# Attention scores from two float32r levels in 64 rows of the array, with neighbouring products in opposite row halves

## The reference, cut to what matters

```python
q = (x @ Wq.T + bq).reshape(B, S, H, Dh).transpose(0, 2, 1, 3)   # 16 heads of 16
scores = jnp.einsum('bhqd,bhkd->bhqk', q, k) / math.sqrt(Dh)
# + slope of the head * (key - query), causal mask, softmax, @ v, @ Wo
```

## Time and profile before

| | us |
|---|---|
| median of 3 runs | 5928.72 |
| lowest, highest | 5915.18, 5933.72 |
| span of the profiled execution | 5916.1 |
| first attention's steps (`ba`) | 833 to 1700 |
| second attention's steps (`ea`) | 3325 to 5150 |

### The profile page before, as it was taken

One profiled execution on the slowest core, in us unless ns is written; L12 is line 12 of the kernel. 1 busy time (PEld: TensorE's weight loads), 2 busy tenths in 40 slices (PEclk: granted clock), 3 DMA queues, 4 the chain that ended last, 5 costly groups with the idle time before them and its releaser, 6 DMA issues. The chain is left out here.

```text
span 5916.1 us, 82750 instructions
## 1 busy us (share of the span) xinstructions
PE 5058.1 (85%) x29088; PEld 2711.9 (46%) x29088; DVE 3390.4 (57%) x6345; ACT 2567.7 (43%) x5102; POOL 1828.3 (31%) x1800
## 2 busy tenths in 40 slices
PE   6566489999978566499987999999999999799996
PEld 3455333333325455357973333333333333255896
DVE  7511468887846721241119788878888878343111
ACT  2311217776662311132215176766766766513221
POOL 2388311111101288534331122222222222104332
PEclk9778779999989687699998899999999999889998
DMA  3476561222213277606986411221221221120798
GB/s 107 116 148 149 138 171 33 62 58 68 62 53 104 76 156 151 149 26 212 330 269 198 108 37 40 63 49 40 64 47 40 64 48 40 55 69 1 267 318 268
DMA packets 503528, 659.28 MB, mean 111 GB/s; under 512 B 147310, under 2 KB 358318, under 8 KB 497998
## 3 DMA queue, kind: packets, MB, share of 16 engines
q1 hardware_dynamic: 370158, 500.99, 27.0%
q0 software_dynamic: 133056, 154.15, 13.2%
HBM read 489.33 MB, written 164.20 MB: 110 GB/s over the span
## 5 line engine op out<-in xcount | busy, mean ns | idle before, releaser
L1724 DVE TENSOR_REDUCE ea_mx<-ea_psA 128x1 f32<-128x512 f32 (+3 forms) x2304 | 1373.9, 653 | 242.0 <-PE ea_psA L1585 144.1
L1706 ACT ACTIVATE ea_pr<-ea_psB 128x512 f32<-128x512 f32 (+3 forms) x2560 | 1198.9, 535 | 567.4 <-PE ea_psB L1608 557.7
L1585 PE MATMUL ea_psA<-ex_kx,ex_qx 99*128 99x512 bf16 (+3 forms) x2560 | 868.4, 357 | 20.2 <-DVE ea_mx L1724 13.3
L1608 PE MATMUL ea_psB<-ex_qx,ex_kx 99*128 99x512 bf16 (+3 forms) x2560 | 846.2, 349 | 0.0
L1724 DVE TENSOR_REDUCE ba_mx<-ba_psA 128x1 f32<-128x512 f32 (+3 forms) x1152 | 686.2, 653 | 144.3 <-PE ba_psA L1585 95.6
L1706 ACT ACTIVATE ba_pr<-ba_psB 128x512 f32<-128x512 f32 (+3 forms) x1280 | 601.5, 536 | 288.9 <-PE ba_psB L1611 155.5
L1625 PE MATMUL ea_psO<-ea_pr,ea_vx 128*32 128x512 f32 (+3 forms) x5120 | 603.5, 543 | 20.9 <-POOL ea_pr L1554 14.0
L1585 PEld LDWEIGHTS ea_psA<-ex_kx,ex_qx 99*128 99x128 bf16 x2560 | 250.3, 98 | 551.8 <-DVE ea_mx L1724 427.8
L1585 PE MATMUL ba_psA<-bx_kx,bx_qx 108*128 108x512 bf16 (+3 forms) x1280 | 443.5, 364 | 7.8 <-PEq L1146 4.5
L1608 PE MATMUL ba_psB<-bx_qx,bx_kx 108*128 108x512 bf16 (+3 forms) x1280 | 424.9, 349 | 14.6 <-DMA bx_qx<-ba_mT 14.4
L1608 PEld LDWEIGHTS ea_psB<-ex_qx,ex_kx 99*128 99x128 bf16 x2560 | 246.5, 98 | 310.3 <-ACT ea_pr L1706 141.0
(11 more groups left out here) (528 smaller groups left out, 8260.9 us busy)
## 6 DMA issues: line engine op xcount, KB each, us to landing
de_wg<-in_L_rg SPq DMA_DIRECT2D x64, 512.0 KB, 4.7
de_wu<-in_L_ru SPq DMA_DIRECT2D x64, 512.0 KB, 5.9
de_wd<-in_L_rd SPq DMA_DIRECT2D x64, 512.0 KB, 7.3
fe_wg<-in_L_rg SPq DMA_DIRECT2D x64, 512.0 KB, 4.9
fe_wu<-in_L_ru SPq DMA_DIRECT2D x64, 512.0 KB, 5.9
fe_wd<-in_L_rd SPq DMA_DIRECT2D x64, 512.0 KB, 7.5
ae_w<-in_L_w SPq DMA_DIRECT2D x64, 384.0 KB, 3.6
ce_w<-in_L_w SPq DMA_DIRECT2D x64, 384.0 KB, 3.8
```

The source lines that it names most:

```text
L1585: last = nc.tensor.matmul(psA[:, slot, at:at + n], qx[0:KB, s, hh, t * P:(t + 1) * P], kx[0:KB, s, hh, k:k + n], start=True, stop=not diag)
L1608: last = nc.tensor.matmul(psB[:, slot, off:BLK], kx[0:KB, s, hh, kt * P:(kt + 1) * P], qx[0:KB, s, hh, Q * BLK + off:(Q + 1) * BLK], start ...
L1706: nc.scalar.activation(pr[:, j % 4, hh, off:BLK], psB[:, exp_slot(n), off:BLK], ACT.Exp).then_inc(s_exp, 1)
L1724: v.tensor_reduce(out, src, AX.X, ALU.max).then_inc(s_ar, 1)
```

## The change

- q and k are split in two float32 values instead of three bf16: `lev[0]` is written by ACT as float32r, `lev[1]` is the rest. Three pairs of levels make 48 rows (`KP`). The bias takes 6 rows in `ba`, 2 in `ea`: 54 and 50 rows.
- Heads lie in row halves: head hh has the rows from `hh % 2 * 64` and the column block `hh // 2` of `qx` and `kx`. Both products of a head are float32r matmuls over 54 or 50 rows that start at row 0 or 64.
- The order of heads is 1, 3, 0, 2 for B (`HEAD_ORDER`) and 0, 2, 1, 3 for A; two heads that share an item are h and h + 2, which lie in the same half.
- Every mask is two matmuls over 64 rows instead of one over 128.
- The maxima get two levels: DVE's chain has 3 instructions instead of 5; the transpose and its copy are float32.
- `load_queries` has 8 DMAs a step; `load_keys` 8 in `ba`, 6 in `ea` (8 in its first two steps).
- The constants `c_q`, `c_k`, `c_q1`, `c_k1` become float32 and are copied from input to scratch in DRAM at the start of the program, on SP's queue behind x and the other constants. `first_operands` on POOL waits for these copies.

```diff
-LEVEL_PAIRS = ((0, 0), (0, 1), (0, 2), (1, 0), (1, 1), (2, 0))
-KP = len(LEVEL_PAIRS) * DH
+Q_LEVELS, K_LEVELS = (0, 0, 1), (0, 1, 0)
+KP = len(Q_LEVELS) * DH
+HALF = P // 2
...
-        lev = sc.sb("lev", [P, NL, 3, BLK], BF16)
+        lev = sc.sb("lev", [P, NL, 2, BLK], F32R)
...
-                    nc.vector.tensor_tensor(res[:, u, :], t32[:, u, :], lev[:, v, 0], ALU.subtract).then_inc(s_c, 1)
-                    dve.wait_ge(s_c, base + n * 2 + 1)
-                    nc.vector.tensor_copy(lev[:, v, 1], res[:, u, :]).then_inc(s_c, 1)
-                    dve.wait_ge(s_c, base + n * 2 + 2)
-                    nc.vector.tensor_tensor(lev[:, v, 2], res[:, u, :], lev[:, v, 1], ALU.subtract).then_inc(s_lo, 1)
+                    nc.vector.tensor_tensor(lev[:, v, 1], t32[:, u, :], lev[:, v, 0].bitcast(F32),
+                                            ALU.subtract).then_inc(s_lo, 1)
...
-            out += [(t, k0, m, (h, h + 1)) for h in (0, 2)] if m <= BLK // 2 else [(t, k0, m, (h,)) for h in range(HV)]
+            out += [(t, k0, m, (h, h + 2)) for h in (0, 1)] if m <= BLK // 2 else [(t, k0, m, (h,)) for h in (0, 2, 1, 3)]
...
+HEAD_ORDER = (1, 3, 0, 2)
...
 def load_queries(eng, op, st, s, signal):
...
+    for half in range(2):
+        at = half * HALF
+        signal(eng.dma_start(op.qx[at:at + op.F, s].bitcast(F32), op.constant(op.qc, st, half)))
+        at += op.F
+        for level in Q_LEVELS:
+            signal(eng.dma_start(op.qx[at:at + DH, s].bitcast(F32), level_rows(op.lvq, level, st, half)))
+            at += DH
...
                 def maxima(i, s, slot):
...
-                        last = nc.tensor.matmul(psA[:, slot, at:at + n], qx[0:KB, s, hh, t * P:(t + 1) * P],
-                                                kx[0:KB, s, hh, k:k + n], start=True, stop=not diag)
+                        r0 = hh % 2 * HALF
+                        last = nc.tensor.matmul(psA[:, slot, at:at + n], qx[r0:r0 + KB, s, hh // 2, t * P:(t + 1) * P],
+                                                kx[r0:r0 + KB, s, hh // 2, k:k + n], start=True, stop=not diag)
                         if diag:
-                            last = nc.tensor.matmul(psA[:, slot, at + n - P:at + n], C["identb"], C["maskA"],
-                                                    start=False, stop=True)
+                            for x in range(2):
+                                last = nc.tensor.matmul(psA[:, slot, at + n - P:at + n], C[f"identb{x}"][r0:r0 + HALF],
+                                                        C[f"maskA{x}"][r0:r0 + HALF], start=False, stop=x == 1)
...
                 def scores(j, hh, st, s, first):
...
+                    head = HEAD_ORDER[hh]
+                    r0, diag = head % 2 * HALF, r >= 0 and not two
+                    last = nc.tensor.matmul(psB[:, slot, off:BLK], kx[r0:r0 + KB, s, head // 2, kt * P:(kt + 1) * P],
+                                            qx[r0:r0 + KB, s, head // 2, Q * BLK + off:(Q + 1) * BLK],
+                                            start=True, stop=not diag)
...
+            for n, dst in kept.items():
+                sp.dma_start(dst.rearrange("r j s -> r (j s)"), D[n].rearrange("r j s -> r (j s)")).then_inc(s_kept, 16)
...
+def two_levels(a):
+
+    a = np.asarray(a, np.float32)
+    top = (a.view(np.uint32) & np.uint32(0xFFFFF000)).view(np.float32)
+    return top, a - top
```

More of the change, by code:

```diff
@@ L14 @@
 BF16 = mybir.dt.bfloat16
+F32R = mybir.dt.float32r
 I32 = mybir.dt.int32
@@ L1368, in load_keys @@
-def load_keys(pool, op, st, s, signal):
[L1369 to L1378, removed]
+        self.of_step = of_step
@@ new lines, in __init__, with keys_in, keys_after, constant @@
+        self.NQ = 2 * len(Q_LEVELS) + 2
+    def keys_in(self, st):
+        return 2 * len(K_LEVELS) + (2 if st < 2 or self.of_step else 0)
+    def keys_after(self, st):
+        return sum(self.keys_in(n) for n in range(2 - st % 2, st + 1, 2))
+    def constant(self, a, st, half):
+        return a[ds((st * 2 + half) * self.F, self.F)] if self.of_step else a
+def level_rows(lv, level, st, half):
+    if len(lv) == 2:
+        return lv[half][level, ds(st * (2 * DH), 2 * DH), :].rearrange("(j d) s -> d j s", d=DH)
+    return lv[0][level, ds(st * (HV * DH), HV * DH), :].rearrange("(j q d) s -> q d j s", q=2, d=DH)[half]
@@ new lines, in load_queries @@
+def load_queries(eng, op, st, s, signal):
+    for half in range(2):
[5 more added lines that the diff above has]
+            at += DH
+def load_keys(pool, op, st, s, signal):
+    for half in range(2):
+        at = half * HALF
+        if st < 2 or op.of_step:
+            signal(pool.dma_start(op.kx[at:at + op.F, s].bitcast(F32), op.constant(op.kc, st, half)))
+        at += op.F
+        for level in K_LEVELS:
+            signal(pool.dma_start(op.kx[at:at + DH, s].bitcast(F32), level_rows(op.lvk, level, st, half)))
+            at += DH
@@ L1607, in scores @@
                     slot = exp_slot(n)
-                    last = nc.tensor.matmul(psB[:, slot, off:BLK], kx[0:KB, s, hh, kt * P:(kt + 1) * P],
-                                            qx[0:KB, s, hh, Q * BLK + off:(Q + 1) * BLK], start=True, stop=two or r < 0)
-                    if r >= 0 and not two:
-                        last = nc.tensor.matmul(psB[:, slot, off:off + P], C["identb"], C["maskB"],
-                                                start=False, stop=True)
+                    head = HEAD_ORDER[hh]
[3 more added lines that the diff above has]
+                                            start=True, stop=not diag)
+                    if diag:
+                        for x in range(2):
+                            last = nc.tensor.matmul(psB[:, slot, off:off + P], C[f"identb{x}"][r0:r0 + HALF],
+                                                    C[f"maskB{x}"][r0:r0 + HALF], start=False, stop=x == 1)
                     last.then_inc(s_b, 1)
@@ L1982, in bf16 @@
     return np.asarray(a, np.float32).astype(mybir.dt.np(BF16))
-def three_levels(a):
-    a, out = np.asarray(a, np.float32), []
-    for _ in range(3):
-        out.append(bf16(a))
-        a = a - out[-1].astype(np.float32)
-    return out
-BIAS_ROWS, BIAS_MAX = 12, 3
+def two_levels(a):
+    a = np.asarray(a, np.float32)
+    top = (a.view(np.uint32) & np.uint32(0xFFFFF000)).view(np.float32)
+    return top, a - top
+BIAS_ROWS = 6
 F32_CONSTS = (("ident", P), ("code", NT), ("dummy", 1), ("ecol1", E0), ("lower", NG0 * NG0), ("rev1", E1),
```

123 lines of the change are left out of this document (53 added, 70 removed).

## The result

The changed kernel takes 6050.89 us (median of 4 runs, 6047.87 to 6073.81) beside 5930.74 us of the kernel before on the same chip: 1.0227 times as long, 95% interval 1.0207 to 1.0248. Forecast were 5705 us. From the first V group to the last, `ba` takes 846.9 us instead of 850.6 and `ea` 1855.8 instead of 1738.9: of the 132 us by which the two profiled executions differ (6047.8 and 5916.1), 117 lie in `ea`'s steps. (Before, `ba`'s last V group ends at 1738 us; the 1700 in the table of times is where its A items end.)

What follows compares the result with a forecast made beforehand. PE was taken to set the pace at 110.4 us a step, DVE 16 to 18 us behind. Steps 229 us less, copies +10, projections -5: 224 less than 5928.7, so 5705 us; range 5580 to 6110, likeliest case 5600 to 5800.

Steps and rivals of the forecast that it cites:

- the sum of a step: Attention steps: PE work, edges and lockstep give 100.5 us in `ea`, 101.6 in `ba`, from 110.4; 229 us less in all.
- what would make it wrong: Signs against the forecast, among them the granted clock (0.99 in middle steps) falling once DVE is level with PE.
- The halves run at once: A and B products in opposite row halves overlap: columns occupy 47.4 us a step in `ea`, 53.9 in `ba`.
- A float32r column: Both products: one float32r instruction of 512 columns takes 0.215 us, like bf16; upper end 0.86.
- no overlap: Rival, attention steps: halves do not overlap, masks and edges remain, +131 us, 6060 us; chance 0.18.
- dear columns: Rival, both products: float32r costs more than bf16; at 0.43 us for 512 columns +880, 6810 us; chance 0.12.
- the estimated 1.54: Speedup of two row halves by the Trainium skill's share: 70% of the overlap's saving, 5755 us; left out of the sum.
- a load waits for the product of its own half: Rival, products' weight loads: a pair takes 0.215 + 0.112 us, about half the overlap lost, 5850 us; chance 0.13.
- PE and DVE in lockstep: Attention steps, three banks: DVE holds PE up, adding 4 us a step in `ea` and 2 in `ba`.
- Edges: PE's steps: three more shape changes a step, in and out, at M's transposes: 6 x 0.095 us, 0.6 us.
- Masks: PE's steps: each mask becomes two in one half, adding 3.5 us a step in `ea`, 6.9 in `ba`.
- Outside: Outside the steps: constant copies at the start cost 10 us, projections gain 5 us.

Runs made afterwards that it cites:

- Clean (5): Changed kernel with GpSimd's scaling in the second attention at unit 25 instead of 14, merges from unit 28 instead of 23: 5918.95 us, ratio 0.9996.
- 3: Changed kernel with the second attention's scaling at unit 21 and every product and mask reading rows 0 to 63, so no opposite halves: 8752.69 us.
- 2: Kernel before, with the second attention's inverses one unit earlier (9 instead of 10) so that GpSimd's scaling meets DVE's chain: 5916.32 us, ratio 0.9996.
- 9: Kernel before, with GpSimd's scaling in the second attention at unit 21 and merges from unit 25: 5905.38 us, ratio 0.9972.
- 12: Changed kernel, scaling still at unit 14, products over all 64 rows of their half, the added rows zeros: 5983.88 us, ratio 1.0100.
- 13: Clean, with products over all 64 rows of their half, the added rows zeros: 5900.0 us, ratio 0.9968.
- 8: Kernel before, in bf16, both products over only the first 54 (ba) or 49 (ea) of their rows: 8264.64 us.
- 6: Clean, with each mask again one bf16 product over 128 rows instead of two over 64: 7394.69 us, ratio 1.2478.
- 10: Clean, with two V groups together in every second unit instead of one in every unit: 6248.78 us, ratio 1.0553.
- 11: Clean, with the order of heads 0, 2, 1, 3 for B as for A: 5984.85 us, ratio 1.0092.
- 4: Changed kernel with scaling at unit 21, plus a final phase of 48 wait-free products of each kind: float32r 512 columns 0.227 us, opposite halves 0.113 to 0.118.
- 7: Clean, with DVE reducing only every second column of the scores: 5760.61 us, 158 less than clean.

## Why the prediction was wrong

**Two things failed.** The result lies 346 us above the forecast. Clean (5) lies 214 us above it, with hardly a fall of the clock: the sum of a step at full clock was too low. The other 132 us go with the falls of the clock and the waits ahead of them, which the sum left out; they turned a change that was worth nothing into a loss.

**The failed step that made it slower is the clock.** The sum of a step multiplied columns by prices at full clock, as the earlier trace rows had it at 0.99, and named a fall only among what would make it wrong, with DVE level with PE as the reason. What the runs show instead: the change halves the rows that a column works in (50 of 128, 99 before), and without the overlap (3) the clock is at 1.2 GHz throughout. With the overlap a wait of 1.3 to 3.3 us goes with 14 to 55 us at 1.2 GHz, where one of 2.5 to 3.9 us cost the kernel before 3 to 7 (2 and above), and one of 1.2 to 2.3 us nothing (2, 9). Waits of 1.3 us or more also come in nine steps of fourteen instead of five, since DVE's chain now meets GpSimd's scaling more often. Take the waits away (5) and the ratio falls from 1.0227 to 0.9996, 132 us between the medians; keep the waits and give every product more rows (12) and it falls to 1.0100, 67 us; do both (13) and the clock stays full. Half rows in bf16 (8), without a wait, stood at 1.2 GHz for most of the attention. Waits aren't the only occasion: in 6, 10 and 11 the clock falls with none of 1 us. What brings it down there no run took apart. The trace of before held the pieces: four falls behind waits, and DVE's chain held for 4.5 us once. I looked at means of five steps, not at the low stretches.

**Right.** The halves run at once, fully in 4, and pairs start 0.01 us apart in the kernel. A float32r column costs what the prediction took, plus 5%. So the rivals of no overlap and of dear columns fall. That the former named 6060 us, 9 from the result, is chance: its mechanism isn't there. Two halves give 2.0 (0.227 to 0.1135 us in 4), not the estimated 1.54. The 5755 us worked out from it leave out the 4 and 2 us for lockstep that 5705 holds; with them it would have been 5835. That a load waits for the product of its own half (the Trainium skill, "TensorE: Matmul & The Clock Gate", "The mechanism") is not so in a running stream: 0.227 us in one half with loads between. At the start of a burst a load does seem to show, below.

**Mis-sized at full clock.** Clean steps are 107.4 and 108.0 us where the sum gave 100.5 and 101.6. Most steps of `ea` before that have no long wait take 108.5 to 109.9 us from V group to V group, so at full clock 1 to 2 us are left of the 9.9 forecast. With DVE's work halved (7) the steps take 100.9 and 103.2, where PE's own sum gave 96.5 and 99.6: some 4 us of each step were missing in PE's work, and 2.5 to 3 in the lockstep.
- *PE and DVE in lockstep*, taken as 4 and 2 us: cutting DVE's work gives 6.5 and 4.9 back (7). The clean step has DVE at 85%. No run cut DVE's work in the kernel before, so how much of this it paid already isn't known.
- *Edges*, taken as 0.6 us. PE of the clean kernel in order of time, two pairs, a V group, and the pairs behind it:

```profile
4000.42 0.49 PE L1594 MATMUL ea_psA<-ex_kx,ex_qx 50*128 50x512 f32 x1 [0.32 <-DVE ea_mx L1738]
4000.43 0.49 PE L1620 MATMUL ea_psB<-ex_qx,ex_kx 50*128 50x512 f32 x1
4000.85 1.07 PE L1639 MATMUL ea_psO<-ea_pr,ea_vx 128*32 128x512 f32 x8
4001.84 0.50 PE L1594 MATMUL ea_psA<-ex_kx,ex_qx 50*128 50x512 f32 x1
4001.85 0.73 PE L1620 MATMUL ea_psB<-ex_qx,ex_kx 50*128 50x512 f32 x2
4002.18 0.39 PE L1594 MATMUL ea_psA<-ex_kx,ex_qx 50*128 50x512 f32 x1
```

  The last product before V takes 0.42 us to V's start (median; 0.31 in the earlier trace rows), and the first pair behind V 0.34 instead of 0.227. Each is 0.11 us more, as much as one float32 load takes, so a load seems to stand bare at each end. Forty V groups make 8.8 us a step. That is more than the 4 us missing in PE's work; what offsets part of it I did not take apart.
- *Masks*: by PE's starts, 3.4 us more in `ea` and 4.9 in `ba`; taken as 3.5 and 6.9.
- *Outside*: 17 us up to `ba`'s first product, taken as 5 in all.

The steps (16 x 6.9 + 8 x 6.4) and the outside (12) make 174 of clean's 214 us; the other 40 I can't assign. What the change is worth with its waits removed and its rows filled is 0.3% (13), as much as moving the scaling gives the kernel before (9).

What stays open: `ba`, with half the rows too, lost nothing. It has no collision, no wait of PE above 0.7 us in these steps, and more masks in a step; no run gave the changed `ba` a wait of 3 us. And why, in the changed kernel, low stretches of much the same waits last 14 to 17 us or 51 to 55.

## What to carry to other kernels

Before cutting the rows of TensorE's work, look at what the granted clock does behind the existing waits: sum its low stretches, and find the wait ahead of each. A matmul that uses less of the array is no faster when the clock halves, so such a change needs its waits removed first, and the clock read again after every change of order (6 and 10 lost it without a long wait). And where two engines stand as close as here (DVE 85% busy in PE's step) over a short ring of buffers, much of a gain on one can be lost at the other: price it by halving the other's work.

## What the hardware showed that I had not expected

- PE 100% busy with products over 49 to 54 rows in one half ran at 1.2 GHz for 3160 us (3) and 2148 us (8), though 8 also has 232 us at 2.4 GHz; the same columns over 99 rows run at 0.99 of 2.4 GHz.
- Rows of zeros count: 64 instead of 50 rows, 14 of them zeros, cut the low stretches from 314 to 140 us (12).
- A VectorE instruction of 0.18 us over 128x16 was held for 4.05 us by a GpSimd product of two SBUF tensors that had started first.
- One 128-row matmul in a stream of 64-row ones costs some 0.3 us beside its own columns (6).
